# First two layers of a four-layer network: the second half's preparation steps are issued ten steps after the first half's

## What is computed

```python
x = x + conv_l(layernorm over channels of x)
t = tokens of x                    # 9216 tokens of 64 channels
t = t + ffn_l(layernorm of t)      # 8 experts, each token uses two
```

## Time and profile before

| | |
|---|---|
| median of 3 runs | 2053.25 us (2052.39 to 2055.82) |
| profiled execution, its own time | 2052.43 us |
| its span, first to last instruction | 2050.0 us |
| mean granted PE clock over the span | 0.821 of full |
| pair of layer 0, to the first dense matmul | 0 to 168.1 us |
| pair of layer 1, to the first dense matmul | 366.4 to 511.4 us |
| busy over the span: PE, DVE, ACT, POOL | 71%, 82%, 63%, 46% |

### The profile page before, as it was taken

The page is one execution under the profiler, slowest core; times in us unless marked ns, Lnnn a source line. Parts: engine busy times, 40 slices in busy tenths (PEclk is TensorE's granted clock), DMA queues, the critical chain, the costliest instruction groups (busy, mean ns, idle before and its releaser), DMA issues.

```text
span 2050.0 us, 47395 instructions
## 1 busy us (share of the span) xinstructions
PE 1463.0 (71%) x16020; PEld 1091.2 (53%) x16020; DVE 1689.1 (82%) x2916; ACT 1282.2 (63%) x2361; POOL 935.6 (46%) x899
## 2 busy tenths in 40 slices
PE   3658989526777776788339999996331449999994
PEld 2544444515333343444238888885220248888883
DVE  5676788697778767888669999999868869999998
ACT  1026989313898867689218888887320128888883
POOL 1003778100222211257117777656215757777653
PEclk9856899676899877789559999998555569999997
DMA  7000000000000100000001111210300011111212
GB/s 321 1 0 28 2 29 2 0 0 0 29 29 29 48 10 1 1 18 27 12 8 42 41 43 43 81 31 11 129 0 16 22 32 41 42 41 40 79 33 97
DMA packets 49469, 74.97 MB, mean 37 GB/s; under 512 B 13636, under 2 KB 34235, under 8 KB 46590
## 3 DMA queue, kind: packets, MB, share of 16 engines
q1 hardware_dynamic: 28354, 42.26, 6.7%
q0 software_dynamic: 20896, 29.73, 4.3%
HBM read 39.88 MB, written 33.08 MB: 36 GB/s over the span
## 4 chain that ended last, share of the span: by engine, by line
PE 36%; DVE 17%; issue 4%; ACT 3%; DMA 0%; POOLq 0%; POOL 0%; DVEq 0%; SPq 0%; ACTq 0%
PE bank L1806 13%; PE bank L1807 10%; PE bank L1823 5%; PE bank L1825 3%; DVE tmp L1161 2%; DVE x L1446 2%; PE bank L1678 1%; PE bank L1527 1%; PE bank L1777 1%; DVE xn L983 1%; DVE st L981 1%; DVE tmp L1134 1%; ACT hl L848 1%; DVE act L1435 1%; DVE xn L1002 1%
## 5 line engine op out<-in xcount | busy, mean ns | idle before, releaser
L688 POOL TENSOR_TENSOR x<-x,ysb 128x256 f32<-128x256 f32 x248 | 230.8, 931 | 639.8 <-DVE ysb L1452 622.5
L635 POOL DMA_INDIRECT rows<-rowsb,pos x288 | 307.5, 1068 | 207.6 <-DVE pos L1290 121.0
L848 ACT ACTIVATE hb<-bank,bias_sb 128x512 f32<-128x512 f32 x432 | 316.2, 732 | 99.7 <-PE bank L1733 52.1
L674 POOL DMA_INDIRECT y<-w,ids x256 | 283.7, 1108 | 138.0 <-DVE w L1359 73.1
L1806 PE MATMUL bank<-xT,uA_ 128*114 128x256 f16 x960 | 255.0, 283 | 5.7
L1807 PE MATMUL bank<-xT,uB_ 128*114 128x256 f16 x960 | 254.2, 277 | 0.0
L1806 PE MATMUL bank<-xT,gA_ 128*114 128x256 f16 x960 | 251.4, 288 | 3.5
L1369 DVE TENSOR_TENSOR act<-bank,act 114x512 f32<-114x512 f32 x320 | 219.9, 687 | 37.8 <-PE bank L1807 15.7
L865 ACT ACTIVATE act<-bank 114x512 f32<-114x512 f32 x320 | 191.1, 597 | 85.7 <-PE bank L1807 76.6
L1807 PE MATMUL bank<-xT,gB_ 128*114 128x256 f16 x960 | 238.1, 274 | 0.0
L1823 PE MATMUL bank<-dW_,hl 114*128 x1920 | 228.8, 220 | 3.0 <-DVE hl L1373 3.0
(11 more groups left out here) (384 smaller groups left out, 3463.1 us busy)
## 6 DMA issues: line engine op xcount, KB each, us to landing
stage<-up SPq DMA_DIRECT2D x8, 1368.0 KB, 7.4
xs<-rows SPq DMA_DIRECT2D x160, 65.0 KB
rows<-land POOLq DMA_DIRECT2D x8, 1137.5 KB, 16.5
rows<-rowsb,pos POOLq DMA_INDIRECT x288, 2.3
y<-w,ids POOLq DMA_INDIRECT x256, 2.3
stage<-down SPq DMA_DIRECT2D x2, 1368.0 KB
rowsb<-y SPq DMA_DIRECT2D x4, 640.0 KB, 5.8
x<-tokens SPq DMA_DIRECT2D x2, 1152.0 KB, 7.3
```

The source lines that it names most:

```text
L635: pool.indirect_dma_start(rows_d[l - SPARSE], bass.IndirectOffsetOnAxis(pos[h][:, k, j:j + 1], 0), words(h)[:, j * RW // 2:(j + 1) * RW // ...
L674: pool.indirect_dma_start(y_d, bass.IndirectOffsetOnAxis(ids[:, t * SUB + u:t * SUB + u + 1], 0), ysb[r][:, u * C:(u + 1) * C], None, boun ...
L688: pool.tensor_tensor(xv, xv, tg[u % 2], ALU.add).then_inc(s["added"], 1)
L848: ins = a.activation(dst[:, 0:SPAN * P], PB[w % 3][:, :], ACT.Gelu, scale=1.0 / WSCALE, bias=b1T[l][:, at:at + 1])
```

## The change

A constant `LAG` of ten steps. In `side_by_side` the second half is carried to step s - 10 when the first half is at step s, on every engine. The waits with written-out counts get their counts from a new helper `nth`, which counts how many increments of both halves come up to a given one in the new order. `side_by_side` is used for layers 0 and 1 alone; for later layers the counts are what they were.

```diff
+LAG = 10
...
+        def nth(steps, h, i):
+
+            return sum((x + LAG * g, g) <= (steps[i] + LAG * h, h) for g in range(HALVES) for x in steps)
+
         def xn_at(n, norm, p):
 
             l, h = divmod(n, HALVES)
-            return 2 * NP * HALVES * l + (NP * (HALVES * norm + h) if l < SPARSE else NP * (2 * h + norm)) + p + 1
+            done = nth((LN1 + 8, LN2 + 8), h, norm) if l < SPARSE else 2 * h + norm + 1
+            return NP * (2 * HALVES * l + done) - (NP - 1 - p)
 
         def turned(l, h, b):
 
-            return HALVES * (len(TB) * l + b) + h + 1
+            return HALVES * len(TB) * l + nth([ROUTE + 2 * k + 1 for k in range(len(TB))], h, b)
 
         def gains(l, h, i):
 
-            return HALVES * ((0, 2)[l] + i) + h + 1
+            steps = ([CONV + 33, CONV + 35], [CONV + 8 + 2 * k for k in range(8)])[l]
+            return HALVES * (0, 2)[l] + nth(steps, h, i)
+
+        def lows_split(l, h):
+
+            return HALVES * NP * l + nth([ROUTE + 5, ROUTE + 7], h, NP - 1)
+
+        def rows_turned(l, h, b):
+
+            return HALVES * NXB * l + nth([ROUTE + 16 + 2 * k for k in range(NXB)], h, b)
 
         def side_by_side(a_, b_, at=LAST, aside=None):
 
             for step in range(LAST):
                 a_.upto(step)
-                b_.upto(step)
+                b_.upto(step - LAG)
                 if step == at:
                     aside.upto(LAST)
...
-            counted = {"t_done": turned(SPARSE, 0, 0) - 1, "res_read": 0, "gain_read": gains(1, 0, 8) - 1}
+            counted = {"t_done": HALVES * len(TB) * SPARSE, "res_read": 0, "gain_read": gains(1, 1, 7)}
...
-                        pe.wait_ge(s["split_lo"], NP * HALVES * l + HALVES * (NP - 1) + h + 1)
+                        pe.wait_ge(s["split_lo"], lows_split(l, h))
...
-                                pe.wait_ge(s["xt_done"], HALVES * (NXB * l + b - 1) + h + 1)
+                                pe.wait_ge(s["xt_done"], rows_turned(l, h, b - 1))
```

## The result

The changed kernel took 2073.52 us (median of 6 runs, 2067.19 to 2080.45) beside 2053.39 for the one before (6 runs), a ratio of 1.0099 with a 95% interval of 1.0082 to 1.0115. Measured a second time (experiment 12) it was 2076.75 beside 2055.63, ratio 1.0103 (1.0082 to 1.0124). The forecast of 2074 and its range held.

| us | before | after | after, second profile |
|---|---|---|---|
| pair of layer 0 | 168.1 | 174.8 | 171.9 |
| dense part of layer 0 | 198.3 | 198.6 | 192.2 |
| pair of layer 1 | 145.0 | 165.6 | 165.6 |
| from there to the end | 1538.6 | 1532.1 | 1539.2 |
| span | 2050.0 | 2071.1 | 2068.8 |

A forecast was written before the change was run, and what follows sets the result against it. DVE's unchanged work plus its waits was taken to bound the two pairs. Layer 0's +5 and layer 1's +16 gave +21 on 2052.43 us, 2073.4, and with the median 0.8 higher 2074 us; range 2060 to 2085.

The forecast's parts named there:

- What bounds the pairs: Paired preparations of layers 0 and 1: no engine is full; length is DVE's unchanged work plus what DVE waits.
- Layer 0, +5 within +2 to +12: Pair of layer 0: DVE's waits sum to +2 us at PE's present level, up to +12 with lowered level; +5 taken.
- logits: Router logits (L1196) in each pair: nothing covers either half's, two waits of 7.9 us, 15.8 instead of 11.4, +4.4.
- the second half's sums: Layer 0, between the first half's iterations: wait 3.6 us instead of 3.2; with the second half's covariance +2.0.
- Layer 1, +13 to +20, took +16: Pair of layer 1: DVE's waits +10 to +15.6 us, plus the pair's end and ACT table loads; +16 taken.
- pooled sums: Layer 1: waits of 3.6 us for the first half and 4.9 for the second, 8.5 instead of 10.1, -1.6.
- The L1015 waits: Layer 1's groups: nine waits lose cover, eight of 1.1 to 1.7 us; 9.5 to 15 in all against 0.3.
- What follows each pair is unchanged and starts later by the same amount: Stretches behind both pairs: pair losses carry to the total in full, 5 + 16 = +21 us; weights loaded far ahead.
- Rival 3: PE at half throughout, kept there by gaps the lag opens: pairs +12 and +20, 2084 us; chance 20%.
- Rival 1: PE's level rises in all six logits and pooled sums, saving 22 us against +15: 2046 us; chance 5%.
- Rival 2: Loss cancelled: three or four of the six logits and pooled sums find the level up; 2053 to 2057 us; 7%.
- Rival 4: Second half catches up in the long waits, shortening L1015's waits, not the logits': some +13, 2066 us; 13%.

The follow-up runs named there:

- experiment 12: The changed kernel again, unaltered, for a second profile and more times: 2076.75 us beside 2055.63 for the kernel before, ratio 1.0103.
- experiment 1: Changed kernel with the ten-step lag in layer 0 alone, layer 1 in lockstep: ratio 1.0002 to the kernel before; pair of layer 0 172.0 us.
- experiment 6: Changed kernel with the ten-step lag in layer 0 alone, run again for a second profile: 2051.27 us beside 2054.54 for the kernel before, ratio 1.0000.
- experiment 11: Changed kernel with the lag in layer 1 alone, plus six spare PE matmuls after every parameter-spreading group there: 2072.87 us beside 2054.54, ratio 1.0097.
- experiment 2: Changed kernel with the ten-step lag in layer 1 alone, layer 0 in lockstep: ratio 1.0108 to the kernel before; pair of layer 1 165.7 us.
- experiment 10: Changed kernel with lag 0, plus five spare PE matmuls after each block of router transposes in layers 0 and 1: 2052.96 us beside 2055.43, ratio 0.9997.
- experiment 7: Changed kernel with a lag of one step instead of ten in both layers: 2045.48 us beside 2055.43 for the kernel before, ratio 0.9957.
- experiment 8: Changed kernel with a lag varying along each pair, 9 or 8 steps at first, 1 from step 46: 2032.48 us beside 2055.43, ratio 0.9897.
- experiment 5: Changed kernel with lag 0, plus four spare DVE sums ahead of layer 0's first step: 2060.92 us beside 2055.43 for the kernel before, ratio 1.0030.

## Why the prediction was right, and where it was wrong

- **What bounds the pairs** (DVE's work plus its waits): right. DVE's work in layer 0 is unchanged, and the waits account for layer 1: 15.6 us more of them, 4.3 up to the second half's L1222, mostly the ten softmax instructions of the first half that now stand ahead of it (3.5 us by themselves), and 0.7 at the end, 20.6 in all.
- **Layer 0, +5 within +2 to +12**: right for the pair, +6.7 and +3.7 (+3.9 and +3.7 in experiments 1 and 6). Step by step: the first half's sums 1.85 or 0.39 (0.6 foreseen), covariances 7.06 and 6.73 (7.1 and 6.7 foreseen), logits 7.96 and 8.03 (7.9), the second half's sums 5.49 or 4.74 (3.6 at the full level; PE was at half for at least part of them), and a bare wait of 1.74 for the second half's first gate group that the prediction did not list. The sum has no term for the pair's end: the rows came 9.9 us later there (6.9 in the second profile), and only because the wait for the bias row had room for 3.2 us of it did the pair lose about what DVE lost. That was not foreseen.
- **Layer 1, +13 to +20, took +16**: the mis-sized term. Normalisation, pooled sums (3.88 and 5.15; 3.6 and 4.9 foreseen), L1092's cover (0.33; 0.2), logits and the order of the first half's second normalisation came as said. The L1015 waits came at their upper end, 14.6 of "9.5 to 15", since PE stood at 0.50 in nearly all of them where "about half of these groups" had been put there: between 2 and 3 of the missing 4.6 us. The end of the pair brought 0.7 where the middle of the forecast is 0.1, the stretch with the softmax 4.3 in place of 3.9; the rest are differences of half a us and less. The terms' upper ends add up to 20.6, which the prediction wrote as 20, so the pair lies just above the stated range. Experiment 11 measured the price of the level: 1.81 against 1.10 a group.
- **"What follows each pair is unchanged and starts later by the same amount"**: the step that failed. The instructions are unchanged, the time is not: 192 to 204 us in the dense part of layer 0. By experiments 1 and 6 the whole doesn't notice layer 0's lag, and experiment 2 carries the whole loss (1.0108). Nor were the weights all there far ahead: before, the first dense matmul of layer 0 waited for the bias row. So the right total came from a term that was 4.6 too small in layer 1 and one of 5 in layer 0 that the whole didn't pay. That the two errors cancel is luck; that the loss is there and where it comes from is not.
- **Rival 3** (PE at half throughout): it happened in layer 1, at its price (+20 foreseen, +20.6), though the whole stayed below its 2084 us (2085 with the 0.8 us that the 2068 beside it contains). The rows agree with the rule cited there from the Trainium skill (TensorE: Matmul & The Clock Gate, the section on how HAM oscillation bites in real kernels): with the gaps that the lag opened, the groups ran at 0.50 from 376 to 430 and from 437 us on, where lockstep had 1.00 from 411 to 430. **Rivals 1 and 2** (the level rises in logits and pooled sums) didn't happen: all six ran at 0.50 in the changed kernel. But experiments 10 and 11 show that it can: 5.3 us for one half's logits and 4.1 for one half's pooled sums, when PE has work right up to them. **Rival 4** (the lag doesn't hold) falls with the four waits of 1.81.
- **The reach of the conclusion**: ten steps is the loss, not a lag as such. Experiments 7 and 8 are faster than lockstep by the same accounting of covers.

**Open**: why the dense part of layer 0 falls into its short form (192 us) in three of four profiles with layer 0's lag, and in none of the seven in lockstep or with the delay. By the times both kernels have executions of both kinds, so chance isn't excluded. Experiment 5, where a delay was paid in full, speaks against a general give-back.

## What to carry to other kernels

When two halves share in-order queues, list for each wait which instruction of the other half covers it, and choose the offset wait by wait: a constant offset long enough for the longest wait lays bare all the short ones (here ten short ones cost 14.6 us in layer 1, and the long one that was covered gave 4 to 5 in layer 0). Here the second half alternated step by step through the short waits, and moved only where a long wait had room; that gave 16 to 23 us where the constant lag cost 20. And before a loss in one stage is carried to the total, look how much the following stage varies by itself.

## What was not expected of the hardware

The same dense instructions took 191, 197 and 203 us at mean granted clocks of 0.94, 0.90 and 0.87, and one program shows more than one of these. In both profiles of the changed kernel the level falls about 23, 58 and 92 us into the dense part of layer 0; it stays down for some 3, 10 and 17 us in the first and 3 each time in the second. The last of the three places, by stretch, 90 to 102 us after ACT's first activation there, in the first profile and then in the second:

```profile
266.00:278.00 12.00, 9.64 (x76) 4.35 (x76) 8.42 (x15) 6.55 (x11) 6.59 (x7) 0.52 0.32 117
```

```profile
263.00:275.00 12.00, 11.18 (x134) 5.46 (x134) 9.98 (x20) 10.15 (x18) 8.24 (x9) 0.86 0.33 117
```

76 matmuls in one, 134 in the other, out of the same queue. And 36 small fp32 matmuls run at the level that they find: the pooled sums (128x4) took 7.8 us after a pause and 4.1 right behind other work, the logits (128x16) 7.7 and 5.3.
